# Layer 1's attention: its first loads issued a phase earlier, a shorter lead-in, and another order of its transfers

## The reference

```
def _L1_xattn_ref(query, key, value, Wq, bq, Wk, bk, Wv, bv, Wo, bo):
    ...
    NUM_HEADS = 16
    HEAD_DIM = ATTEN_DIM // NUM_HEADS
    ...
    q = query @ Wq + bq
    k = key @ Wk + bk
    v = value @ Wv + bv
    ...
    scale = 1.0 / HEAD_DIM ** 0.5
    scores = jnp.einsum('bqhd,bkhd->bhqk', q, k) * scale
    attn = jax.nn.softmax(scores, axis=-1)
    out = jnp.einsum('bhqk,bkhd->bqhd', attn, v)
    ...
    return out @ Wo + bo
...
x = x + _L1_xattn_ref(_layernorm(x, axis=-1), ctx_1024, ctx_1024, ...)
```

## Time and profile before

| | |
|---|---|
| median of 3 runs | 4438.6 us |
| the profiled execution's own time | 4427.33 us |
| its span | 4425.5 us |
| PE, DVE, ACT, POOL busy share of the span | 92%, 63%, 63%, 19% |
| TensorE's mean granted clock, as a share of full | 0.959 |
| L1a's first instruction and its last transpose (line 546) | 385.2 us and 1131.5 us |
| PE's first instruction of L1a | 394.7 us |
| DVE's scaling of weights and biases (lines 686 to 695) | 395.84 to 397.37 us |
| first `tops` of the lead body | 434.2 us |
| line 513 of batch 0's group 0, with which the body of batch 0 begins | 455.5 us |

### The profile page before, as it was taken

One profiled execution on the slowest core, in us unless ns is written; L12 is line 12 of the kernel. 1 busy time (PEld: TensorE's weight loads), 2 busy tenths in 40 slices (PEclk: granted clock), 3 DMA queues, 4 the chain that ended last, 5 costly groups with the idle time before them and its releaser, 6 DMA issues. The chain is left out here.

```text
span 4425.5 us, 76944 instructions
## 1 busy us (share of the span) xinstructions
PE 4092.8 (92%) x26955; PEld 2929.3 (66%) x26988; DVE 2774.0 (63%) x6291; ACT 2800.3 (63%) x4880; POOL 828.0 (19%) x727
## 2 busy tenths in 40 slices
PE   7897999999889999999999999779999999978799
PEld 6664454454467777777777777547888888855467
DVE  7655878788465656556565655465555555548556
ACT  6423667677256666666666667536777777756457
POOL 2100000000000000000000000006777777751100
PEclk9898899999899999999999999889999999989899
DMA  2101433221100000000000000100000000000000
GB/s 73 37 1 32 76 44 48 38 43 20 44 12 1 12 12 1 13 1 12 1 13 1 12 1 1 42 16 8 8 8 8 8 1 1 1 9 1 34 9 8
DMA packets 79712, 79.33 MB, mean 18 GB/s; under 512 B 10372, under 2 KB 72996, under 8 KB 78220
## 3 DMA queue, kind: packets, MB, share of 16 engines
q1 hardware_dynamic: 74860, 67.97, 7.4%
q10 hardware_dynamic: 4464, 6.30, 0.4%
HBM read 51.31 MB, written 4.19 MB: 13 GB/s over the span
## 5 line engine op out<-in xcount | busy, mean ns | idle before, releaser
L2446 POOL TENSOR_TENSOR L3a_p_lo<-L3a_wq,L3a_p_hi 128x512 fp32r<-128x512 f32 (+1 forms) x480 | 623.4, 1310 | 262.8 <-ACT L3a_p_hi L2396 252.8
L1283 DVE CUSTOM_DVE_ANT_0 L2a_sc<-L2a_score,L2a_mask_n 128x804 f32<-128x804 f32 x512 | 499.0, 991 | 102.5 <-issue 73.7
L1186 ACT ACTIVATE L2a_pt<-L2a_ring 128x512 f32<-128x512 f32 x768 | 431.0, 598 | 178.3 <-PE L2a_ring L1072 176.6
L621 ACT ACTIVATE L1a_work<-L1a_ring 128x1024 f32<-128x1024 f32 x416 | 412.5, 1026 | 169.1 <-PE L1a_ring L439 168.1
L742 DVE TENSOR_REDUCE L1a_mx<-L1a_ring 128x2 f32<-128x1024 f32 x384 | 456.5, 1222 | 60.8 <-PE L1a_ring L458 56.8
L1072 PE MATMUL L2a_ring<-L2a_ident,L2a_sc 128*128 128x128 f32 x3072 | 437.1, 280 | 5.9 <-ACT L2a_sc L1171 1.9
L1171 ACT ACTIVATE L2a_sc<-L2a_sc,L2a_nb 128x1608 f32<-128x1608 f32 x256 | 417.2, 1632 | 0.7 <-DVE L2a_nb L1288 0.7
L2534 DVE TENSOR_REDUCE L3a_mx<-L3a_ring 128x1 f32<-128x402 f32 (+2 forms) x640 | 316.3, 538 | 145.3 <-PE L3a_ring L2248 137.5
L1072 PEld LDWEIGHTS L2a_ring<-L2a_ident,L2a_sc 128*128 128x128 f32 x3072 | 343.2, 142 | 80.3 <-issue 42.3
L2395 ACT ACTIVATE L3a_wq<-L3a_ring 128x512 f32<-128x512 f32 (+1 forms) x480 | 283.8, 591 | 159.7 <-PE L3a_ring L2170 102.7
L1087 PE MATMUL L2a_res<-L2a_pt,L2a_v 128*64 128x256 f32 (+1 forms) x3328 | 373.4, 381 | 1.6 <-ACT L2a_pt L1186 1.6
(11 more groups left out here) (749 smaller groups left out, 9068.9 us busy)
## 6 DMA issues: line engine op xcount, KB each, us to landing
L1a_keys<-L1a_k_hi SPq DMA_DIRECT2D x224, 52.0 KB
L1a_cx<-in_ctx SPq DMA_DIRECT2D x8, 768.0 KB
L2a_cx<-in_ctx SPq DMA_DIRECT2D x8, 768.0 KB
L1a_keys<-L1a_k_lo SPq DMA_DIRECT2D x112, 52.0 KB
L0a_cx<-in_ctx SPq DMA_DIRECT2D x16, 320.0 KB, 3.7
L3a_cx<-in_ctx SPq DMA_DIRECT2D x16, 320.0 KB, 3.4
L2a_mask_u<-in_mask SPq DMA_DIRECT2D x16, 200.1 KB, 4.4
L1a_scr_q<-L1a_keys SPq DMA_DIRECT2D x3, 1024.0 KB
```

Of the source, the lines that this page charges most:

```text
L621: act.activation(probs[:, (par * NU + u) % c.PS, :, :], ring[tile][:, :, :], ACT.Exp).then_inc(tile_free[tile], 1)
L1186: ins = act.activation(pt[:, t:t + 4, g // 3, q], bank[:, :].rearrange("p (t q) -> p t q", t=4), ACT.Copy)
L1283: dve.tensor_tensor_reduce(sc[:, two, e, w].rearrange("p (k j) -> p k j", k=2), score[e][:, :, 0:CH], mask_n[:, r % 2, w].rearrange("p (k ...
L2446: pool.tensor_tensor(p_lo[0:r, at % PL, 0:W], probs[0:r, at % 2, 0:W], p_hi[0:r, at % PH, 0:W].bitcast(F32), ALU.subtract).then_inc(part_o ...
```

## The change

**Loads.** A class `HeadsAhead` holds L1a's weights and the context tile. Phase L0f calls its `begin` on SP: the first 12 row tiles of context 0 and the 15 weight transfers are issued there, behind L0f's own last load. The context's last 65 rows follow at the start of L1a. ACT issues none of them any more.

**Start.** Only group 0 is prepared ahead of the lead body: four key pieces, one transpose of x (batches 0 and 1 are in it), group 0's queries. DVE norms 4 of 16 row tiles, POOL computes the reciprocal roots and norms the other 12. DVE clears only the 24 columns of padding of the value tiles instead of all.

**The rest, beside the lead body.** `HeadsPlan.rest` lists 14 pieces: four of the plain keys (`high`), three transposes of x, four of the queries of all batches, three of batch 0's own queries (groups 1 to 3). One stands behind each of the 14 `tops` of group 0, on PE, ACT and DVE. All 14 use the one PSUM bank `res`, and a piece starts on PE when the one before it has left the bank (`rest_free`).

**Transfers.** Batch 0's groups 1 to 3 are no longer computed on PE. They are copied by 36 transfers of 52 KB from the plain keys, as for the other batches, behind four transfers of the constant rows. Only then come the write of the queries to DRAM, the constant rows of the second tile, the queries of batch 1, and the keys of batch 1. The third context (batch 2) is loaded behind these keys, not ahead of them.

```diff
+        tops = [n for kind, off, n in self.order if kind == "tops" and n[0] == 0]
+        self.rest = [("high", k) for k in range(self.KB)] + [("turn_x", k) for k in range(1, 4)]
+        self.rest += [("query", k) for k in range(4)] + [("own", g) for g in range(1, self.NG)]
+        self.beside = dict(zip(tops, self.rest))
...
+class HeadsAhead:
...
+        self.loads = [(self.ident, io["ident"]), (self.bkr, a("bkr")), (self.wkr, a("wkr")), (self.bqr, a("bqr")),
+                      (self.cols, io["cols"]), (self.wqr, a("wqr")), (self.wq, a("wq")), (self.bq, a("bq")), (self.wk, a("wk")),
+                      (self.bk, a("bk")), (self.wv, a("wv")), (self.bvg, a("bvg")), (self.wfin, a("wfin")),
+                      (self.pick, io["pick4"]), (self.bo, a("bo"))]
+
+    def context(self, sp, n, got):
+        sp.dma_start(self.cx[:, 0:CT - 1, :],
+                     self.ctx_dram[n, 0:(CT - 1) * P, :].rearrange("(t p) d -> p t d", p=P)).then_inc(got, 16)
+
+    def begin(self, sp):
+        self.context(sp, 0, self.c_first)
+        for tile, dram in self.loads:
+            sp.dma_start(tile[:], dram).then_inc(self.w_in, 16)
...
-        first = [("turn_c", k) for k in range(KB)] + [("key", (0, k)) for k in range(KB)] + [("turn_x", k) for k in range(QC)]
-        first += [("key", (g, k)) for g in range(1, NG) for k in range(KB)] + [("own", g) for g in range(NG)]
-        first += [("query", k) for k in range(QC)]
+        first = [("turn_c", k) for k in range(KB)] + [("key", (0, k)) for k in range(KB)] + [("turn_x", 0), ("own", 0)]
         first_at = lambda kind, n: first.index((kind, n))
+        rest_at = lambda kind, n: c.rest.index((kind, n))
+        highs = [s for s in c.rest if s[0] in ("high", "query")]
...
+                early = isinstance(n, int) and n == 1
+                if more and not early:
                     sp.wait_ge(aux_free, c.aux(n, "turn_c", KB - 1) + 1)
                     load_context(n + 1)
                 if not (isinstance(n, int) and n < 2):
                     sp.wait_ge(oraw_ok, n * NG - NG)
                 replicate(n, par)
+                if early:
+                    load_context(n + 1)
...
             sp.wait_ge(zero_ok, 1)
-            load_context(0)
-            for tile, dram in loads[0::2]:
-                sp.dma_start(tile[:], dram).then_inc(w_in, 16)
+            load_tail(0)
             sp.wait_ge(pre_full, KB)
             load_context(1)
-            sp.wait_ge(ql_ok, QC)
+            sp.wait_ge(keys_ok, KB)
+            for r in range(4):
+                at = slice(32 * r + 3 * c.DH, 32 * r + 32)
+                sp.dma_start(keys[at, 0, 1:NG, :].bitcast(F32),
+                             keys[at, 0, 0:1, :].bitcast(F32).broadcast_to([c.DH, NG - 1, JP])).then_inc(const_first, 16)
+            sp.wait_ge(rest_free, rest_at("high", KB - 1) + 1)
+            for g in range(1, NG):
+                replicate_keys(g, 0)
+            sp.wait_ge(rest_free, rest_at("query", QC - 1) + 1)
             for copy, rows in enumerate((q_hi, q_hi, q_lo)):
                 sp.dma_start(scr_q[:, copy].rearrange("r d g j -> r (d g) j"), rows.bitcast(F32)).then_inc(q_put, 16)
             sp.wait_ge(q_put, 48)
             sp.wait_ge(blank_ok, 1)
             for r in range(4):
                 at = slice(32 * r + 3 * c.DH, 32 * r + 32)
-                sp.dma_start(keys[at, 1, :, :].bitcast(F32), keys[at, 0, :, :].bitcast(F32)).then_inc(const_in, 16)
+                sp.dma_start(keys[at, 1, :, :].bitcast(F32),
+                             keys[at, 0, 0:1, :].bitcast(F32).broadcast_to([c.DH, NG, JP])).then_inc(const_in, 16)
             prepare(1, 1)
...
+            def rest(kind, n):
+                at = rest_at(kind, n)
+                if at:
+                    pe.wait_ge(rest_free, at)
+                else:
+                    pe.wait_ge(bias_ok, 1)
+                if kind == "high":
+                    w = span_of(n)
+                    pe.matmul(res[:, 0:w.stop - w.start], wk[:, :], kt[:, w], start=True, stop=True).then_inc(rest_full, 1)
+                elif kind == "own":
+                    own(res, n, rest_full)
+                elif kind == "turn_x":
+                    pe.wait_ge(xp_ok, n)
+                    turn_x(res, n, rest_full)
+                else:
+                    pe.matmul(res[:, :], wq[:, :], yt[:, n * 512:(n + 1) * 512], start=True, stop=True).then_inc(rest_full, 1)
...
+            pe.wait_ge(w_in, W_ALL)
+            pe.wait_ge(ahead.c_first, 16)
             for k in range(KB):
+                if k == KB - 1:
+                    pe.wait_ge(c_got, 16)
                 first_turn_c(k)
             for k in range(KB):
                 first_key(0, k)
-            pe.wait_ge(xn_ok, 1)
-            for k in range(QC):
-                first_turn_x(k)
-            for g in range(1, NG):
-                for k in range(KB):
-                    first_key(g, k)
-            pe.wait_ge(pre_free, first_at("turn_x", QC - 1) + 1)
-            for g in range(NG):
-                first_own(g)
-            for k in range(QC):
-                first_query(k)
             for g in range(NG):
                 mm = pe.matmul(res[:, 0:1], wfin[:, g, :], bvg[:, g:g + 1], start=(g == 0), stop=(g == NG - 1))
             mm.then_inc(bias_mm, 1)
-            pe.wait_ge(keys_ok, NG * KB)
-            pe.wait_ge(queries_ok, NG)
-            pe.wait_ge(ql_ok, QC)
+            pe.wait_ge(xn_ok, 1)
+            turn_x(claim_first("turn_x", 0), 0, pre_full)
+            pe.wait_ge(const_ok, 1)
+            pe.wait_ge(pre_free, first_at("turn_x", 0) + 1)
+            own(claim_first("own", 0), 0, pre_full)
+            pe.wait_ge(pre_free, len(first))
+            pe.wait_ge(keys_ok, KB)
...
+                if i == 0 and isinstance(b, int) and b == 0:
+                    pe.wait_ge(queries_ok, g + 1)
+                    if g == 1:
+                        pe.wait_ge(const_first, 64)
+                elif i == 0 and g == 0:
+                    pe.wait_ge(q_in, b * 64)
+                    if isinstance(b, int) and b == 1:
+                        pe.wait_ge(const_in, 64)
                     pe.wait_ge(k_in[g], b * 192)
+                if i == 0 and g:
+                    pe.wait_ge(k_in[g], b * 192 + 192)
...
+                if isinstance(b, int) and b == 0 and n in c.beside:
+                    rest(*c.beside[n])
...
+            def tops(b, par, n):
+                if not (isinstance(b, int) and b == 0 and n in c.beside):
+                    return
+                kind, k = c.beside[n]
+                act.wait_ge(rest_full, rest_at(kind, k) + 1)
+                if kind == "high":
+                    w = span_of(k)
+                    act.activation(k_hi[:, w], res[:, 0:w.stop - w.start], ACT.Identity, bias=bk[:, 0:1],
+                                   scale=1.0).then_inc(rest_high, 1)
...
+            turn_x(first_full("turn_x", 0), 0, pre_free)
+            own(first_full("own", 0), 0, pre_free)
...
+            pool.memset(half[:, :], -0.5)
             pool.memset(one[:, :], 1.0)
+            pool.drain()
+            for n, (t0, t1) in enumerate(((0, 4), (4, NT))):
+                pool.wait_ge(mv_ok, n + 1)
+                rsqrt_chunk(pool, st, half, slice(t0, t1)).then_inc(rs_ok, 1)
+            pool.drain()
+            for k in range(1, QC):
+                norm_chunk(pool, xn, x, st, range(4 * k, 4 * k + 4)).then_inc(xp_ok, 1)
...
+            stats_chunk(dve, x, st, range(4)).then_inc(mv_ok, 1)
+            dve.wait_ge(w_in, W_ALL)
...
-            rsqrt_steps(dve, st["rs"][:, :], st["var"][:, :], st["tmp"][:, :], NT)
-            apply_norm(dve, xn, x, st, NT).then_inc(xn_ok, 1)
+            stats_chunk(dve, x, st, range(4, NT)).then_inc(mv_ok, 1)
+            dve.wait_ge(rs_ok, 1)
+            dve.drain()
+            norm_chunk(dve, xn, x, st, range(4)).then_inc(xn_ok, 1)
...
+            def rest(kind, n):
+                if kind == "high":
+                    w = span_of(n)
+                    dve.wait_ge(rest_high, highs.index((kind, n)) + 1)
+                    dve.scalar_tensor_tensor(k_lo[:, w], res[:, 0:w.stop - w.start], bk[:, 0:1], k_hi[:, w].bitcast(F32), ALU.add,
+                                             ALU.subtract).then_inc(rest_free, 1)
+                elif kind == "own":
+                    dve.wait_ge(rest_free, rest_at(kind, n) + 1)
+                    merge_queries(n)
+                elif kind == "query":
+                    w = slice(n * 512, (n + 1) * 512)
+                    dve.wait_ge(rest_high, highs.index((kind, n)) + 1)
+                    dve.scalar_tensor_tensor(q_lo[:, w], res[:, :], bq[:, 0:1], q_hi[:, w].bitcast(F32), ALU.add,
+                                             ALU.subtract).then_inc(rest_free, 1)
+
+            for k in range(KB):
+                first_key(0, k)
+            dve.wait_ge(pre_free, first_at("own", 0) + 1)
+            merge_queries(0)
...
```

(13 more changed lines are left out.)

148 lines of the change are left out of this document (68 added, 80 removed).

## The result

The changed kernel takes 4456.4 us (median of 17 executions, 4446.8 to 4468.6), the kernel before 4435.5 us (17, 4431.5 to 4450.9). The ratio is 1.0042, with a 95% interval of 1.0034 to 1.0050: 15 to 22 us slower, 18.6 by the ratio and 20.9 by the two medians. The forecast was +18, as a median 4456.6. That the two medians agree to 0.2 us is luck: the forecast stands on a median of 4438.6 (3 executions) for the kernel before, which is 4435.5 over 17.

The account below looks back on a forecast made before the run. The start was taken as bound by PE's idle wait for weights, then DVE and ACT; the change makes SP's queue bind. Context 2's transposes +16.0 and restart +2 gave +18 on 4438.6, 4456.6 us, range 4448.6 to 4462.6 (62%).

Parts of the forecast that it names:

- The start: L1a up to the first `tops`: earlier loads and less preparation put it at about 403.4 for 434.16, 30.8 us earlier.
- The lead body: First `tops` to line 513: 14 added pieces, plain keys or queries 3.3 us each, make it 42.7 us for 21.3.
- rival 1: Clock rises in the lead body and the queue is freer: context 2 lands at 542.7, +6.4 us, 4445.0; chance 15%.
- SP's chain: SP's queue after the plain keys: 33.6 + 34.8 + 17.5 + 44.1 + 5.3 us, ending with context 2 at 552.3.
- The middle: Constant transfers and batch 1's query reads on SP's queue, ahead of the 48 key copies: 17.5 us, bounds 12.9 and 22.1.
- the landing: Context 2 as last entry of SP's queue: 4.3 us for 0.8 MB at 185 GB/s, 5.3 with its latency.
- rival 2: The chain hides: copies issue at 0.68 us each, landing at 527, the start's 9.4 us stay, 4429.2; chance 12%.
- The waits: PE waits some 14 us at batch 1's first `tops`, then 7 to 12 us at context 2's transposes, 16.0 us later than before.
- The restart: PE behind the wait for context 2: low clock costs 2 us, taken from 0 to 4.2.

## Why the prediction was right, point by point

**The start.** First `tops` 401.2, predicted 403.4. The 30.8 us were 32.9. The stretches were as worked out: DVE took 8.6 us from its clearing to the end of the norm (384.64 to 393.26, predicted 386.69 to 395.4), and from there to the first `tops` it was 8.0 us, as predicted. Only the beginning was off: 1.3 us because L1a began earlier, the rest because the gap of 0.86 us ahead of the clearing was gone. POOL's 12 tiles were hidden (395.1 to 405.0).

**The lead body.** 40.7 us (401.23 to 441.88), predicted 42.7. The plain keys were complete at T = 412.3, predicted 417.0: 2.2 us of that from the start, 2.5 from here, 11.1 us for 13.6. This term was mis-sized: I took a pitch of 3.3 us at the low clock for all of them, and the queries' pieces (line 456 of PE) stood 3.6 us apart at one clock and 2.7 at the other, those of the plain keys (line 449) 2.7:

```profile
405.59 1.13 PE L449 MATMUL L1a_res<-L1a_kt,L1a_wk 128*128 128x512 f32 x2
408.28 1.12 PE L449 MATMUL L1a_res<-L1a_kt,L1a_wk 128*128 128x512 f32 x2 [1.13 <-DVE L1a_k_lo L795]
...
416.84 2.08 PE L456 MATMUL L1a_res<-L1a_work,L1a_wq 128*128 128x512 f32 x2
420.48 2.08 PE L456 MATMUL L1a_res<-L1a_work,L1a_wq 128*128 128x512 f32 x2 [0.84 <-DVE L1a_keys L803]
424.92 1.15 PE L456 MATMUL L1a_res<-L1a_work,L1a_wq 128*128 128x512 f32 x2
427.63 1.12 PE L456 MATMUL L1a_res<-L1a_work,L1a_wq 128*128 128x512 f32 x2 [1.13 <-DVE L1a_keys L803]
```

```profile
404.00:432.00 28.00, 20.91 (x73) 10.12 (x71) 16.81 (x19) 9.48 (x22) 2.75 (x3) 0.80 0.41 50
```

The granted clock from 404 to 432 was 0.80, a mean of both levels (1.00 from 408 to 412, 0.50 from 416 to 424), so rival 1's first half came true: its T was 412.

**SP's chain.** 36 copies 32.5 us (33.6), write 34.2 (34.8), constants and queries 20.0 (17.5, within 12.9 to 22.1), 48 copies 43.6 (44.1), context 7.6 to its landing (5.3). In all 137.9 for 135.3. The middle and the landing (whose 1 us of latency no row had shown) were undersized, together by 4.8 us, which copies and write, 2.2 us shorter, and T, 4.7 us earlier, more than made good: the context was there at 550.2, predicted 552.3. Rival 1 needed 12.9 in the middle, and rival 2 a pace of 0.68 us per copy; it was 0.91 (43.6 / 48).

**The waits.** 16.0 us at batch 1's first `tops` (predicted 14) and 7.6 at context 2's transposes (7 to 12). Here too two misses met: batch 1's first copy was issued 3.9 us earlier than the 502.9 of the sum, but from the end of the 12th copy's issue (510.0) to PE's start it was 3.7 us, where I had 1 us to land, which no row had shown. That the second wait sets the end is shown by the two kernels with the context elsewhere, which lose it alone and are 7 and 8 us faster, 12 at the mark, and by the one with the shorter write, which loses the first alone and still ends with the second.

**The restart.** The transposes stood 13.9 us later than before (550.18 for 536.30), where I had 16.0, and 4.4 more were lost behind the second wait, where I had 2 of 0 to 4.2: 18.3 at the mark, 18 predicted. So this term was undersized by 2.4 us and the landing came 2.1 us earlier than predicted, and part of the agreement in the sum is luck. The whole price of 4.2 from the rows would have been nearer than its half. I also read those rows wrongly: the slot of 22.7 us did not run mostly at the low clock, which ended at 465, 9.5 us into it. Here PE ran 11.1 us at 0.50; how much of the 4.4 is clock and how much the refilling of the three PSUM tiles was not separated.

**What stays open.** In the profiled execution 8.8 us more are lost at later batch boundaries, where no new wait stands. Batch 5's first two group slots take 54.7 us (889.40 to 944.08) for 50.3 before:

```profile
889.40:944.08 54.68, 51.43 (x404) 27.00 (x402) 36.76 (x44) 31.88 (x41) 1.90 (x1) 0.84 0.26 44
```

The clock was 0.84 there and 0.97 before, with the same instructions. From the mark to batch 7's last group the kernel with loads alone lost 14 us in its profile against the kernel before, the one with 12 transfers and the context in the write's wait none. Their programs do not differ there, so I take it to differ by execution; with one trace of each kernel that is not shown. Since the kernels lie 18.6 us apart by the ratio and the mark is 18.2 in absolute times, it seems to cancel in the medians; what makes the clock fall there was not tried.

## What to carry to other kernels

Before work is moved off a busy engine onto a queue, add up everything the queue does between the first input and the last user: here 138 us of issues and landings behind one moment, each cheap. A start that is 13 us faster is worth nothing when the queue behind it grows by 23 us, so that its first user is served 10 us later than before. Then look at the longest entry of the queue with its DMA share: here a share of 0.26 with nothing else in the queue was the sign of a transfer that can be cut better, and the recut of that one transfer, with the old place of another, turned 19 us slower into 11 us faster (by the ratios).

## What the runs showed of the hardware that was not expected

- The same 3 MB from SBUF to DRAM took 34.2 us in three transfers with 4 as outermost dimension and 14.6 us in twelve of 32 rows.
- A transfer of 768 KB put ahead of four small ones cost the chain 2 us, not the 9.1 that its issues held the queue: the issues behind it were 7.2 us shorter.
- Transfers on ACT's queue slowed those on SP's from 32.5 to 44.9 us for 36 copies, and an issue on ACT held it for 0.55 to 1.15 us.
- Behind a wait of 16.0 us PE ran 6.7 us at 0.50 before the clock was back at 1.00, behind one of 7.6 us it ran 11.1 us. The longer wait did not cost the longer restart.
